# Attended x in tiles of 8 rows and 16 columns, loaded a second time, and a new order of calls

## The reference

```python
# x: (4, 256, 64, 64) float32
k = conv(x, w1 (128, 256, 7, 7), dilation 2, padding 6) + b1
k = conv(k, w2 (49, 128, 1, 1)) + b2
attn = softmax(k, axis=1)                    # 49 taps per pixel
xp = pad(x, 6)                               # 6 pixels on every side of the image
shifts = stack([xp[:, :, 2*u:2*u+64, 2*v:2*v+64] for u in range(7) for v in range(7)], axis=1)
x = einsum('bkchw,bkhw->bchw', shifts, attn) # attended x
# layer 1: a fixed sequence yc (256 channels x 64 columns) from a small scan
y = gelu(yc + x * D);  out = x + y
out = layernorm over the 256 channels, times ln_w, plus ln_b
```

## Time and profile before

| | us |
|---|---|
| median of 3 runs | 812.79 (812.68 to 813.52) |
| the profiled execution, its own time | 813.03 |
| its span, first to last instruction | 810.9 |
| granted TensorE clock, mean | 0.983 |
| PE busy / DVE / ACT / POOL | 758.2 / 677.6 / 566.1 / 191.0 |
| DMA moved | 41.78 MB in 133598 packets |

### The profile page before, as it was taken

How to read it: one execution, slowest core, us unless ns; L and a number is a source line. 1 busy time by engine, 2 the same in 40 slices (tenths; PEclk the granted TensorE clock), 3 DMA queues, 4 the chain that set the end, 5 groups by cost and what they waited for, 6 DMA issues and landing times.

```text
span 810.9 us, 27182 instructions
## 1 busy us (share of the span) xinstructions
PE 758.2 (93%) x12242; PEld 448.2 (55%) x12242; DVE 677.6 (84%) x867; ACT 566.1 (70%) x917; POOL 191.0 (24%) x102
## 2 busy tenths in 40 slices
PE   4969989999999999999999999999999999997994
PEld 1535545764567545664567545764567455754671
DVE  0898997989888988989888888998888888595765
ACT  2873545768786796678786787678786777568546
POOL 4114113114211341114301431115302421022011
PEclk9979999999999999999999999999999999999988
DMA  9460050001602035201702053201711020201104
GB/s 295 130 105 2 3 93 16 3 1 24 135 4 53 3 77 81 55 2 27 132 2 55 2 107 53 55 2 27 132 27 30 2 53 4 55 2 48 39 22 104
DMA packets 133598, 41.78 MB, mean 52 GB/s; under 512 B 133145, under 2 KB 133226, under 8 KB 133226
## 3 DMA queue, kind: packets, MB, share of 16 engines
q1 hardware_dynamic: 132248, 40.01, 22.2%
q10 hardware_dynamic: 1234, 0.04, 0.1%
HBM read 23.27 MB, written 16.78 MB: 49 GB/s over the span
## 4 chain that ended last, share of the span: by engine, by line
PE 42%; ACT 20%; DVE 17%; issue 5%; POOL 2%; DVEq 0%; ACTq 0%
PE cv L484 20%; PE wk L525 9%; PE wk L544 4%; ACT chs L903 4%; ACT V L860 4%; PE wk L583 3%; POOL chs L371 2%; PE ms L556 2%; DVE o L1507 2%; DVE V L1359 2%; DVE Z L1400 2%; ACT ms L953 1%; DVE XT L1390 1%; DVE chs L1459 1%; DVE o L1520 1%
## 5 line engine op out<-in xcount | busy, mean ns | idle before, releaser
L484 PE MATMUL cv<-V,W 128*32 128x496 f16 (+6 forms) x7840 | 428.2, 374 | 3.6 <-issue 1.9
L484 PEld LDWEIGHTS cv<-V,W 128*32 128x32 f16 (+1 forms) x7840 | 198.8, 96 | 201.4 <-issue 15.3
L860 ACT ACTIVATE V<-R,sc 128x1024 f16<-128x1024 f32 (+1 forms) x88 | 109.6, 1274 | 59.6 <-DVE R L1285 50.7
L346 POOL TENSOR_TENSOR R<-raw 128x1152 f32<-128x1152 f32 x32 | 93.1, 2909 | 205.6 <-DVE V L1359 102.8
L1359 DVE SCALAR_TENSOR_TENSOR V<-R,sc,V 128x1024 f16<-128x1024 f32 (+1 forms) x88 | 115.1, 1328 | 2.6 <-ACT V L860 2.6
L544 PE MATMUL wk<-band,XT 128*128 128x224 f16 (+1 forms) x900 | 97.3, 266 | 0.9
L544 PEld LDWEIGHTS wk<-band,XT 128*128 128x128 f16 x900 | 76.6, 98 | 24.6 <-ACT o L926 6.0
L525 PEld LDWEIGHTS wk<-AT,sel 128*128 128x128 f16 x2368 | 73.5, 100 | 15.0 <-issue 11.0
L525 PE MATMUL wk<-AT,sel 128*128 128x16 f16 x2368 | 77.8, 193 | 0.1
L371 POOL TENSOR_TENSOR chs<-o 128x1024 f32<-128x1024 f32 x14 | 45.1, 3223 | 132.1 <-DVE o L1507 123.1
L1285 DVE SCALAR_TENSOR_TENSOR R<-R 128x1024 f32<-128x1024 f32 (+1 forms) x56 | 70.3, 1287 | 0.0
(11 more groups left out here) (194 smaller groups left out, 916.9 us busy)
## 6 DMA issues: line engine op xcount, KB each, us to landing
raw<-in_x_dram SPq DMA_DIRECT2D x16, 1024.0 KB, 11.3
out_dram<-o SPq DMA_DIRECT2D x28, 512.0 KB, 4.5
w1raw<-in_L_conv_w_dram SPq DMA_DIRECT2D x2, 3136.0 KB, 16.8
out_dram<-o SPq DMA_DIRECT2D x8, 256.0 KB, 3.9
cm<-in_L_conv_Cmat_dram ACTq DMA_DIRECT2D x1, 32.0 KB, 8.3
dcol<-in_L_conv_D_dram ACTq DMA_DIRECT2D x2, 0.5 KB, 10.2
lnw<-in_L_conv_ln_w_dram ACTq DMA_DIRECT2D x2, 0.5 KB, 7.3
lnb<-in_L_conv_ln_b_dram ACTq DMA_DIRECT2D x2, 0.5 KB, 7.4
```

What stands on the lines that cost most here:

```text
L346: nc.gpsimd.tensor_tensor(R[buffer][:, :, :, :], rows_of(par, j + 2), rows_of(par, j), ALU.subtract).then_inc(pool_rows, 1)
L484: ins = pe.matmul(to.rearrange("p (w t c) -> p w t c", w=2, c=COLS)[:, :, :, c0:c1], W[:, ws, h * K7 + v, k0:k1], slot(n, a)[:, low, :, t0 ...
L860: nc.scalar.activation(v_array(n, a, 0), array(a), ACT.Identity, scale=sc[:, par, 3:4]).then_inc(vhi, 1)
```

## The change

A tile of x is now 8 rows by 16 columns of one parity (still 128 pixels, 16 tiles). It reaches 14 output rows of 19 columns. `apply` uses three row blocks of two column blocks, 18 matmuls, of which 12 have 11 x 19 = 209 columns and 6 have 3 x 19 = 57. Before, 15 matmuls had 224, 320 or 96 columns, 1184 per product.

`spread` still has ten steps, now by output columns: eight steps make two columns for both column blocks (28 matmuls of 16 columns), one makes four edge columns (56 matmuls of 8) and one makes two (28 matmuls of 8).

A row block of 16 columns can't be read from `raw` as one pattern, so each pair of tiles is loaded again from DRAM, by two DMAs (one per channel half) of 128 partitions x 8 rows x 128 bytes, into one of three stages: two lie in `AT`, which is free between `spread` and the next `turned_attention`, the third is the new tile `xs`. `fetch_rows` issues them from ACT's queue, 16 DMAs per pass; SP issues the first six of the run. `turn_x` reads the stage and waits for its landing. `raw` is still loaded for the convolution.

The order of calls in `unit` is new on PE, ACT and DVE. The core of the diff:

```diff
-SEL_TAPS = ((0, 7), (3, 7), (2, 7), (1, 7), (0, 6), (0, 5), (0, 4))
+SEL_TAPS = ((0, 7),) + tuple((v, 7) for v in range(1, 7)) + tuple((0, v) for v in range(6, 0, -1))
+SPREAD = tuple(((c, None), (c + 1, None)) for c in range(0, TCOLS, 2))
+SPREAD += (((16, 0), (17, 0), (18, 0), (-3, 1)), ((-2, 1), (-1, 1)))
...
+        xs = sb("xs", [P, HALVES * TROWS * 2 * TCOLS])
+        band = sb("band", [P, 2, 2 * XROWS, BROWS, 2 * BCOLS], F16)
...
+            for g in range(3):
+                for h in range(HALVES):
+                    sp.dma_start(stage(g)[:, h], tile_rows(0, g, h)).then_inc(xs_in[g], 16)
...
-                for j in range(ROWS // 4):
-                    r0, r1 = max(4 * j - PAD, 16 * q), min(4 * j + 4 + PAD, 16 * q + 16)
+                for j in range(XROWS):
+                    r0, r1 = max(TROWS * j - PAD, 16 * q), min(TROWS * j + TROWS + PAD, 16 * q + 16)
...
+                    for e in range(XTILES):
+                        to = out_rows[:, r0 - 16 * q:r1 - 16 * q, (COLS - BCOLS) * e:(COLS - BCOLS) * e + BCOLS]
...
+                k = STAGES * n + g
+                pe.wait_ge(xs_in[k % 3], 32 * (k // 3) + 32)
...
+            def fetch_rows(n, g):
+
+                k = STAGES * n + g
+                if g < 3:
+                    act.wait_ge(sel_done, STEPS * n)
+                    act.wait_ge(xt_done, STAGES * n)
+                else:
+                    act.wait_ge(xt_done, k - 2)
+                for h in range(HALVES):
+                    act.dma_start(stage(k)[:, h], tile_rows(n, g, h)).then_inc(xs_in[k % 3], 16)
```

More of the change, by code:

```diff
@@ L194, in conv_seq_kernel @@
         raw = (raw0, raw1)
+        stages = [AT[:, w, PAD:PAD + ROWS, :].rearrange("p r c -> p (r c)").bitcast(F32) for w in range(2)] + [xs[:, :]]
+        tile_rows = lambda n, g, h: xv[n // 2, n % 2, h][:, TROWS * (g // XTILES):TROWS * (g // XTILES) + TROWS,
+                                                         2 * TCOLS * (g % XTILES):2 * TCOLS * (g % XTILES) + 2 * TCOLS]
+        stage = lambda k: stages[k % 3].rearrange("p (h r c) -> p h r c", h=HALVES, r=TROWS)
         ms = ctx.enter_context(nc.psum_tensor("ms", [P, 2, BANK], F32))
@@ L521, in spread @@
                     pe.wait_ge(blo, 10 * m + r - banks + 1)
[L522 to L527, removed]
+                for k, (c, edge) in enumerate(SPREAD[r]):
+                    v = 3 - c if c < PAD else c - 6 if c > TCOLS - PAD - 1 else 0
+                    for row in range(BROWS):
+                        f = v * SEL_STEP + (BROWS - 1 - row) * TCOLS + BCOLS - 1 - c
+                        last = row + TROWS * (XROWS - 1) + 1
+                        if edge is None:
+                            to = sum_of_step(m, r).rearrange("p (w j r) e c -> p w j r e c", w=2, j=XROWS)[:, :, :, row, :, k]
+                            attention = AT[:, :, row:last:TROWS, c:c + TCOLS + 1:TCOLS]
+                        else:
+                            to = sum_of_step(m, r).rearrange("p (w j r) c -> p w j r c", w=2, j=XROWS)[:, :, :, row, k]
+                            attention = AT[:, :, row:last:TROWS, c + TCOLS * edge]
+                        ins = pe.matmul(to, sel[:, f:f + P], attention, start=True, stop=True)
                 ins.then_inc(sel_done, 1)
@@ L805, in _ @@
             keep_running(2)
-            for r in range(BROWS):
+            for r in range(STEPS):
                 spread(m, r)
@@ L1010, in unit @@
                 attended(m, other, 1)
-                v_high(n, par, 10)
+                fetch_rows(n, 1)
+                fetch_rows(n, 0)
+                fetch_rows(n, 2)
                 sum_2(n, par)
                 attended(m, other, 2)
-                if nxt:
-                    v_high(n + 1, other, 0)
                 attended(m, other, 3)
                 gelu(m, 0, 0)
-                gelu(m, 0, 1)
                 attended(m, other, 4)
                 attended(m, other, 5)
-                gelu(m, 1, 0)
+                gelu(m, 0, 1)
                 attended(m, other, 6)
                 attended(m, other, 7)
+                gelu(m, 1, 0)
                 spread_mean(m, 0)
@@ L1228, in _ @@
             scale_shift(m - 1, 1, 1)
-            for r in range(4, BROWS):
+            for r in range(4, STEPS):
                 band_high(m, r)
```

202 lines of the change are left out of this document (119 added, 83 removed).

## The result

The changed kernel takes **868.64 us** (median of 3 runs, 860.21 to 872.08) against 812.79: 1.066 times as long [1.062, 1.069], 56 us more. The forecast was 823, the range 792 to 842. The profiled execution is the shortest of the three (860.21, mean granted TensorE clock 0.953; the others have 0.936 and 0.938), and before ran at 0.983.

A forecast was written before the change was run, and what follows sets the result against it. PE, busy 758.2 of 810.9 us, was taken to bound the kernel. Seven passes at +1.6 us (+11.2) and the tail at -1 took the span from 810.9 to 821.1; with 2.1 around it, 823 us, range 792 to 842.

The forecast's parts named there:

- Issues on ACT: DMA issues hold ACT's queue, 0.73 us for third and later ones: six in a row 4.0, four 2.5, a pair 1.0.
- PE idle before the fifth quarter: In `apply`, the fifth quarter waits for ACT's third-quarter copy, late behind six issues: 2.7 us of PE idle.
- Second mean: In the layer norm, four issues ahead of the Ln table load: PE idle 3.1 us instead of 0.99.
- First mean: In the layer norm, the mean waits for POOL's sum of 3.34 us: 0.8 us of PE idle.
- The last step of spreading: In spreading, a late ACT copy would make the next step wait, 0.3 us at a time.
- A quarter of `apply`: On PE, 2850 columns and 18 gaps take 1.31 us: -0.29 a quarter, -2.3 a pass.
- rival (d): PE gets nothing in `apply`, short runs stream no faster: 2.3 us more a pass, 830 to 835; chance 0.05.
- the pass, step by step: Walk through one pass: PE's work 2.7 us less, its waiting 4.3 to 5 more, so it ends 1.6 later.
- (a): Issues on ACT are free: about 86.2 us a pass, 786 in all; chance 0.22 for 784 to 802.
- Rival (b): Each issue on ACT costs 0.41, none held up: -0.75 a pass, 806 to 807; chance 0.18 with its neighbourhood.
- (c): Issues on ACT held up in full, 1.21 each: pass +4.5, 843; chance 0.11 with what lies up to it.
- the two table loads: On ACT, Ln and Exp each need a 1.28 us load; by the skill's one-load rule the pass is 1.3 shorter.

The follow-up runs named there:

- e1: Changed kernel with the row loads issued from SP's queue instead of ACT's, same tiles, bytes and order of other calls: 803.6 us, 0.9877.
- e9: e1 with conv(27, 28) called ahead of spread(m, 9) instead of behind it: 795.02 us, 0.9775.
- e8: Changed kernel with 40 matmuls of zeros added ahead of the fifth quarter of `apply` and 40 ahead of the second mean in each unit: 839.79 us, 1.0316.
- e5: Changed kernel with row loads issued from SP's queue and the unit calls in the order of before; new tiles stay: 804.53 us, 0.9885.
- e2: Kernel before with only the new order of calls on PE, ACT and DVE; old tiles, no row loads: 819.79 us, 1.0074.
- e3: Changed kernel with the old order of calls; row loads stay on ACT, six behind the second quarter's copy, the rest in pairs: 839.83 us, 1.031.
- e4: Changed kernel with three convolution steps moved ahead of the fifth quarter of `apply`, issues still on ACT: 859.56 us, 1.056.
- e6: Changed kernel with the four issues of stages 1 and 0 called ahead of attended(m, 0), still on ACT: 830.17 us, 1.0208.
- e7: Changed kernel with the four issues of stages 5 and 6 called behind inverse_deviation(m, 0) and v_high(n + 1, 1), still on ACT: 840.09 us, 1.032.
- e11: e10 with conv(27, 28) ahead of spread(m, 9), as in e9: 799.72 us, 0.9839.
- e12: e1 with eight matmuls of zeros of 112 columns ahead of spread(m, 9), nothing else moved: 799.67 us, 0.9831.
- e10: Changed kernel with the issue moves of e6 and e7 together, all issues still on ACT: 807.24 us, 0.9907.

## Why the prediction was wrong

The direction was right, the size wrong by 46 us: a pass was to be 1.6 us longer and is 7.0 longer. By its own steps:

- **Issues on ACT.** Six 4.0 us forecast; 4.3 in the pass shown, but 4.9 on average. Four 2.5, and 2.9 on average. A pair 1.0, and mostly 1.01. So the mechanism was right and the price of a held-up issue, 0.73, too low. (Its lower bounds, 2.5 and 1.6, are six and four times 0.41 and leave out the 0.62 of the second issue; with it they are 2.7 and 1.9.) The estimate drawn from the Trainium skill ("DMA: Bandwidth & Descriptors", "How a descriptor splits into AXI transactions") had six at 4.9, which is what the seven passes average; whether the start at byte 128 plays a part no run here separated. No tile's landing (2.4 to 4.5 us) was waited for, as forecast.
- **PE idle before the fifth quarter.** 2.7 forecast with ACT's `attended` as releaser; 3.05 in the pass shown, 3.6 on average: +0.9 a pass, as much as the six issues were longer.
- **Second mean.** 3.1 forecast; 3.2 to 4.6, on average 3.7: +0.6. The releaser was as named, `normalise`.
- **First mean.** 0.8 forecast; it doesn't wait in the changed kernel, since PE comes later than I had it and POOL's sum took 2.36 us, not the 3.34 of the earlier trace rows: -0.8.
- **The last step of spreading** waits 0.34 us for DVE in six of the seven passes, a wait that the prediction had named for its walk but left out of the sum: +0.3.
- **A quarter of `apply`.** 1.31 forecast, 1.38 measured at full clock from start to start (e1: six from 343.03 to 351.32), from 1.62 before. Here the arithmetic was wrong and not the assumption: 1.63 less 1.48 us over 15 matmuls is 10 ns each by its own rows, where it wrote 7 to 8; with 10 the sum is 1.37. Runs of 19 columns cost no more per column, and rival (d), no gain at all, is wrong. With the rest of PE's work the gain is 2.2 us a pass (87.84 to 85.62 of e9) where 2.7 was forecast: +0.5.
- **The small ones.** A copy of a step 0.55 us (L981), forecast 0.53; spreading 80.9 us in all for 84.1, 0.4 a pass as forecast; 26 selections 6.1 us for 3.65, hidden. Right.
- **The step that failed: "the pass, step by step" priced waits as idle time only.** After each of its two long waits PE works at half clock for some 3 us. That is in no term and no rival. PE is busy 89.18 us a pass in the changed kernel and 85.62 in e9, with the same matmuls at full clock: 3.6 us a pass, 25 in all. By groups most of it lies in `apply` (97.8 us instead of the 84.9 of e1), then in `mean`, the convolution and the transposes of `turn_x`; the one fall behind spreading is in it too. e8, in which both waits stay and the clock doesn't fall behind them, is 28 us faster. The profile before could not show it: its longest wait in a pass is 1 us, and its clock is even.

The list closes: idle time went from 2.0 to 7.6 us a pass, 5.6 more, where the sum had 4.3: +1.3, of which the four terms above give 1.0. With 0.5 and 3.6 that is 5.4, and 1.6 + 5.4 = 7.0. Six such passes are 42 of the 47 us between the profiled spans; the first begins 2.0 us later (forecast 0, by 2), and 3.4 us lie behind the last `turn_logits`, where the seventh pass has both its waits and is 7.6 us longer, and the tail is 4.1 us shorter (forecast 1). The other two runs have clocks of 0.936 and 0.938, so more of the last term, and the median is 8 us above the profiled run; no trace of theirs shows where.

Of the rivals, (a), issues free, was tested by e1, e5 and e9. It was 786; 804, 805 and 795 came out. e9 is its mechanism almost in full: a pass of 87.2 where (a) said 86.2. The 0.5 of PE's work are missing, and the second mean waits 1.50 instead of 0.99, because one table load does stand in the way, against the forecast: in e9 Ln starts 0.6 us behind the end of `variance`, when the load of its table ends; before it was 0.1. Rival (b) fell on the price of an issue. (c), 843, was the nearest number, mostly for the wrong reason: six issues were to be 5.9 us and were 4.9, and the clock made up the rest and more. What the prediction took for granted, that the rest of the new order is neutral, costs 6 us on the old tiles (e2), most of it by the clock, and gains 9 us on the new once the clock holds (e9 against e5, where e9 has one move of the convolution more).

On the two table loads the trace after decides as before: Ln and Exp take two (L1011, L1016), 1.28 us each, and not the one of the Trainium skill's rule, which stands in "ScalarE: Activation LUTs" under "Table sets: the hidden batching unit". Why the build put two here is left open.

## What to carry to other kernels

In this kernel a wait of PE of 3 us cost 4.5: the idle time, and the half clock behind it. Price a long wait as more than its idle time, and look in the windows for a granted clock of 0.5 before asking what the engines do. Put DMA issues on a queue that nobody waits for, or in a stretch where their engine is idle anyway: two calls earlier was worth 37 us here, and 16 issues a pass then cost next to nothing. A wait moved from PE to the next step of the same ring is not removed.

## What was new of the hardware

- At or behind waits of PE of 3.0 to 4.6 us the granted clock fell to 0.50 in 13 of 14 cases of the changed kernel and in all 27 of e3, e4, e6 and e7; it stayed there for some 3 us in nine of the 13, and for some 7 in four, part of that while PE was idle.
- Shorter waits are safer, not safe. Behind waits of 2.2 us it fell in five of seven cases (e4), behind one of 2.52 (e6), and not behind one of 2.65 (e8). Before the second means with waits of 1.5 to 2.0 it fell in one of seven cases of e3 and two of six of e11, and in none of the 21 of e1, e9 and e12.
- It can fall while PE still waits, up to 2.0 us before PE starts again (after, at 753.5), or up to 1.5 us behind the start (e3).
- Work without any use keeps the clock up: 30 us of zeros bought 28 us net.
- It also fell with PE at work throughout: once in e12, behind 84 matmuls of 16 columns, zeros, and 28 of 8, and once in e10, behind the same without the zeros. What brings it about there is left open; e5, with 84 of 8 columns in a row and no wait ahead, never showed it.
- An issue of 1024 packets holds ACT's queue for at least 0.37 us, 0.60 in the median, and 0.8 on average in a row of six, with single ones up to 2.3.
